# Cumulated decays of a state space scan as selected rows, and where its small copies and scalings run

## What is computed

```python
zxbcdt = jnp.einsum('bld,ed->ble', u, W_in)          # z: 1024, x/B/C: 1024 + 128 + 128, dt: 16 heads
xBC = silu(_causal_depthwise_conv(xBC, conv_w, conv_b))
dt = softplus(dt + dt_bias);  A = -exp(A_log)
def step(h, inp):                                    # h: 16 heads x 64 x 128
    h = h * exp(dt * A)[..] + (dt * x)[..] * B[..]
    y = einsum('bhpn,bn->bhp', h, C)
y = y + D * x
y = y * silu(z)
y = y * rsqrt(mean(y * y) + EPS) * norm_w
return einsum('ble,de->bld', y, W_out)
```

## Time and profile before

| | before |
|---|---|
| median of three runs | 1223.34 us (1223.04 to 1226.01) |
| the profiled execution's own time | 1224.82 us |
| its span | 1223.1 us |
| granted TensorE clock, mean over the span | 0.934 |
| busy: PE, DVE, ACT, POOL | 88%, 70%, 39%, 29% |

### The profile page before, as it was taken

How to read it: one execution, slowest core, us unless ns; L and a number is a source line. 1 busy time by engine, 2 the same in 40 slices (tenths; PEclk the granted TensorE clock), 3 DMA queues, 4 the chain that set the end, 5 groups by cost and what they waited for, 6 DMA issues and landing times.

```text
span 1223.1 us, 14496 instructions
## 1 busy us (share of the span) xinstructions
PE 1072.2 (88%) x4844; PEld 507.3 (41%) x4844; DVE 852.1 (70%) x1164; ACT 471.3 (39%) x706; POOL 354.7 (29%) x166
## 2 busy tenths in 40 slices
PE   7999999699999899789447999999897789996897
PEld 3444444344444344434113444444621144684353
DVE  6577777899999056673862299999366339275696
ACT  2354454566665134136760110100044424334163
POOL 4244544244433013000010377774100000361003
PEclk9999999799999899889768999999979889997898
DMA  6154554432230783020010445453100200000000
GB/s 235 54 168 144 168 177 150 156 106 94 103 103 35 274 310 138 0 87 1 1 69 1 140 158 205 150 206 104 35 1 1 70 2 1 1 1 1 2 1 35
DMA packets 41844, 112.61 MB, mean 92 GB/s; under 512 B 4528, under 2 KB 15312, under 8 KB 35664
## 3 DMA queue, kind: packets, MB, share of 16 engines
q1 hardware_dynamic: 38608, 101.13, 23.7%
q10 hardware_dynamic: 2880, 9.96, 2.4%
q0 software_dynamic: 320, 1.05, 0.3%
HBM read 103.18 MB, written 7.34 MB: 90 GB/s over the span
## 4 chain that ended last, share of the span: by engine, by line
PE 60%; DVE 23%; issue 9%; ACT 7%; DVEq 1%; ACTq 0%; DMA 0%; POOL 0%; SPq 0%; POOLq 0%
PE PS L1502 5%; PE PS L1504 5%; PE PS L1503 5%; PE PS L870 4%; DVE arena L659 3%; PE PS L249 3%; PE PS L250 3%; PE PS L251 3%; PE PS L1570 2%; DVE XN L609 2%; DVE arena L1772 2%; PE PS L744 2%; PE PS L745 2%; PE PS L746 2%; PE PS L1893 1%
## 5 line engine op out<-in xcount | busy, mean ns | idle before, releaser
L714 PE MATMUL PS<-arena 128*128 128x512 f16 x256 | 97.1, 379 | 9.7 <-POOL arena L466 7.6
L744 PE MATMUL PS<-arena 128*128 128x512 f16 x256 | 97.9, 383 | 5.9 <-DVE arena L659 5.9
L491 POOL TENSOR_TENSOR arena<-arena 128x2048 f16<-128x2048 f32 x16 | 70.1, 4381 | 111.4 <-ACT arena L536 105.4
L1502 PE MATMUL PS<-arena 128*128 128x512 f16 x256 | 97.0, 379 | 1.8 <-DVE arena L1393 1.8
L745 PE MATMUL PS<-arena 128*128 128x512 f16 x256 | 97.9, 382 | 0.0
L746 PE MATMUL PS<-arena 128*128 128x512 f16 x256 | 97.8, 382 | 0.0
L715 PE MATMUL PS<-arena 128*128 128x512 f16 x256 | 97.0, 379 | 0.0
L716 PE MATMUL PS<-arena 128*128 128x512 f16 x256 | 97.0, 379 | 0.0
L1503 PE MATMUL PS<-arena 128*128 128x512 f16 x256 | 97.0, 379 | 0.0
L1504 PE MATMUL PS<-arena 128*128 128x512 f16 x256 | 97.0, 379 | 0.0
L659 DVE SCALAR_TENSOR_TENSOR arena<-arena,MASK 128x512 f16<-128x512 f16 (+1 forms) x64 | 96.0, 1500 | 0.1
(11 more groups left out here) (340 smaller groups left out, 2387.0 us busy)
## 6 DMA issues: line engine op xcount, KB each, us to landing
arena<-in_ctxT SPq DMA_DIRECT2D x32, 1024.0 KB, 6.4
arena<-in_ctx SPq DMA_DIRECT2D x16, 1024.0 KB, 5.3
arena<-in_w ACTq DMA_DIRECT2D x8, 1024.0 KB, 5.2
arena<-in_w SPq DMA_DIRECT2D x8, 1024.0 KB, 4.8
XN<-in_ffnGU SPq DMA_DIRECT2D x16, 384.0 KB, 3.3
XN<-in_WinT SPq DMA_DIRECT2D x16, 290.0 KB, 5.0
gu_hi<-arena SPq DMA_DIRECT2D x16, 192.0 KB, 3.4
gu_lo<-arena SPq DMA_DIRECT2D x16, 192.0 KB, 3.5
```

The source lines that it names most:

```text
L714: pe.matmul(bank, CHI[:, b, e, cols], QHI[:, e, :], start=(e == 0), stop=False)
L744: pe.matmul(PS[:, t, :], PHI[:, j, cols], CHI[:, b, j, :], start=False, stop=False)
L1502: pe.matmul(bank, QHI3[:, e, cols], CHI3[:, b, e, :], start=(e == 0), stop=False)
```

## The change

The decays of all heads are first summed over the steps with the heads as rows. POOL fills SELECT, which has for each head a 128-column block with ones in three rows (0, 32 and 64 rows down). DVE copies DTA three times into DTAR, 32 columns apart; four float32 products of PE, now with the two sums ahead of z, put the cumulated decays of the 16 heads, three times, into 96 rows of bank 7. DVE splits them into three bf16 parts (PARTS). In a round, one bf16 product of 512 columns writes the negative numbers for four heads, and for each head one bf16 product of its SELECT block with PARTS adds the decays. ACT, not DVE, copies B. ACT takes a square root of a constant before it waits for the last output, and scales the third and fourth output (after DVE has scaled its first), DVE the first and second. SELECT, PARTS and DTAR have memory of their own; REST lies where the old state's part is kept from the second round on.

```diff
-        DVE_MARK = marks(... "s4_sums_read", "s4_la", "s5_taps", ...)
+        DVE_MARK = marks(... "s4_sums_read", "s4_la", "s4_parts", "s5_taps", ...)
-        POOL_MARK = marks(... "s4_pad", "s4_wout")
+        POOL_MARK = marks(... "s4_pad", "s4_select", "s4_wout")
@@ -1633,6 +1633,10 @@
         LA = view(SMALL + 4096, [3, NT, SSM_H])
         ELA = view(SMALL + 5120, [3, NT, SSM_H])
         NLA = view(SMALL + 2304, [NT, SSM_H])
+        SELECT = view(170 * K, [SSM_H, P], BF16)
+        PARTS = view(174 * K, [N], BF16)
+        DTAR = view(175 * K, [NT, 96])
+        REST = view(159 * K, [N])
         MS = view(SMALL + 3072, [NT])
         RMS = view(SMALL + 3328, [NT])
@@ -1677,6 +1681,15 @@
         def s4_pool(pool, link):
             pool.wait_ge(x_done, NT * 4)
             pool.memset(XBC[:, :, 0:3], 0.0).then_inc(pool_marks, 1)
+
+            link(pool.memset(SELECT, 0.0))
+            for part in range(3):
+                ins = pool.affine_select(out=SELECT, in_=SELECT, compare_op=ALU.not_equal, fill=1.0,
+                                         base=-32 * part, pattern=[[-1, SSM_H], [0, P]], channel_multiplier=1)
+                if part < 2:
+                    link(ins)
+                else:
+                    ins.then_inc(pool_marks, 1)
             pool.wait_ge(act_marks, ACT_MARK["s4_ela"])
             for q in range(NT):
                 if q < NT - 1:
@@ -1732,6 +1745,8 @@
             act.wait_ge(dve_marks, DVE_MARK["s4_la"])
             act.activation(ELA, LA, ACT.Exp).then_inc(act_marks, 1)
             for q in range(NT):
+                act.wait_ge(s4_small, q + 1)
+                act.copy(BNAT, PS[:, 2, 0:P])
                 if q:
                     act.wait_ge(s4_intra, q)
                 for h in range(SSM_H):
@@ -1741,9 +1756,14 @@
                     if h % 4 == 3:
                         ins.then_inc(s4_decay, 1)
             for q in range(NT):
+                if q == NT - 1:
+                    act.activation(COLS[:, 46:47], EPSC[:, 0:1], ACT.Sqrt)
                 act.wait_ge(s4_ys, q + 1)
                 link(act.activation(ZG[:, q, :], YS[:, q, :], ACT.Square, accum_out=MS[:, q:q + 1]))
             act.activation(RMS, MS, ACT.Sqrt, scale=1.0 / SSM_I, bias=EPSC[:, 0:1]).then_inc(act_marks, 1)
+            act.wait_ge(s4_yn, 1)
+            for q in (2, 3):
+                act.activation(YS[:, q, :], YS[:, q, :], ACT.Copy, scale=RMS[:, q:q + 1]).then_inc(s4_yn, 1)
             for c in range(IT):
                 act.wait_ge(s4_yt_psum, c + 1)
                 if c == 0:
@@ -1761,7 +1781,11 @@
             dve.wait_ge(act_marks, ACT_MARK["s4_softplus"])
             link(dve.scalar_tensor_tensor(out=DTV, in0=DTV, scalar=0.0, in1=DTE, op0=ALU.max, op1=ALU.add))
             link(dve.tensor_scalar(ALOG, ALOG, -1.0, None, ALU.mult))
-            dve.tensor_tensor(DTA, DTV, ALOG.unsqueeze(1).to_broadcast([P, NT, SSM_H]), ALU.mult).then_inc(dve_marks, 1)
+            link(dve.tensor_tensor(DTA, DTV, ALOG.unsqueeze(1).to_broadcast([P, NT, SSM_H]), ALU.mult))
+            link(dve.memset(DTAR, 0.0))
+            for part in range(3):
+                ins = dve.tensor_copy(DTAR[:, :, 32 * part:32 * part + SSM_H], DTA)
+            ins.then_inc(dve_marks, 1)
             dve.wait_ge(pool_marks, POOL_MARK["s4_pad"])
             for g in range(CVT):
@@ -1787,6 +1811,14 @@
             link.note(dve.tensor_scalar(NLA, SUMS[:, 0], -1.0, None, ALU.mult))
             link(dve.tensor_tensor(LA[:, 1], SUMS[:, 1], SUMS[:, 0], ALU.subtract))
             dve.sem_inc(dve_marks, 1)
+
+            link(dve.tensor_copy(PARTS[0:96, :], PS[0:96, 7, :]))
+            link(dve.tensor_tensor(REST[0:96, :], PS[0:96, 7, :], PARTS[0:96, :], ALU.subtract))
+            for rows in (slice(32, 64), slice(64, 96)):
+                link(dve.tensor_copy(PARTS[rows, :], REST[rows, :]))
+            rows = slice(64, 96)
+            link(dve.tensor_tensor(REST[rows, :], REST[rows, :], PARTS[rows, :], ALU.subtract))
+            dve.tensor_copy(PARTS[rows, :], REST[rows, :]).then_inc(dve_marks, 1)
             dve.wait_ge(s4_z, 2 * NT)
             for q in range(NT):
@@ -1794,7 +1826,6 @@
                 xs = PS[:, 0:2, :].rearrange("p a (h c) -> p (a h) c", c=SSM_P)
                 dve.tensor_tensor(heads(DTX[:, 0:SSM_I]), xs, DTV[:, q, :].unsqueeze(2).to_broadcast([P, SSM_H, SSM_P]),
                                   ALU.mult).then_inc(s4_dtx, 1)
-                link.note(dve.tensor_copy(BNAT, PS[:, 2, 0:P]))
                 dve.tensor_tensor(heads(YS[:, q, :]), xs, SSMD.unsqueeze(2).to_broadcast([P, SSM_H, SSM_P]),
                                   ALU.mult).then_inc(s4_read, 1)
                 for g in range(4):
@@ -1828,7 +1859,7 @@
             dve.tensor_tensor(YS[:, NT - 1, :], YS[:, NT - 1, :], ZG[:, NT - 1, :], ALU.mult).then_inc(s4_ys, 1)
             dve.wait_ge(act_marks, ACT_MARK["s4_rms"])
             link(dve.reciprocal(RMS, RMS))
-            for q in range(NT):
+            for q in range(2):
                 dve.tensor_scalar(YS[:, q, :], YS[:, q, :], RMS[:, q:q + 1], None, ALU.mult).then_inc(s4_yn, 1)
             for c in range(IT):
                 dve.wait_ge(xt_hi, 2 * DT + c + 1)
@@ -1856,6 +1887,14 @@
                     ins = matmul_split(pe, PS[:, g % 4, :], (WIN_HI[:, c, cols], WIN_LO[:, c, cols]),
                                        (XT_HI[:, c, :], XT_LO[:, c, :]), c, DT)
                 ins.then_inc(s4_conv_psum, 1)
+            pe.wait_ge(dve_marks, DVE_MARK["s4_dta"])
+
+            for k, rows in enumerate((UPPER, ONES)):
+                ins = pe.matmul(PS[:, 6, k * P:(k + 1) * P], rows[:, :], DTVA.rearrange("p t h -> p (t h)"),
+                                start=True, stop=True)
+            for q in range(NT):
+                ins = pe.matmul(PS[0:96, 7, q * P:(q + 1) * P], DTAR[:, q, :], UPPER[:, :], start=True, stop=True)
+            ins.then_inc(pe_marks, 1)
             for g in range(2 * NT):
                 if g >= 2:
                     pe.wait_ge(s4_z, g - 1)
@@ -1865,12 +1904,6 @@
                     ins = matmul_split(pe, PS[:, 4 + half, :], (XT_HI[:, c, rows], XT_LO[:, c, rows]),
                                        (WIN_HI[:, c, cols], WIN_LO[:, c, cols]), c, DT)
                 ins.then_inc(s4_z_psum, 1)
-            pe.wait_ge(dve_marks, DVE_MARK["s4_dta"])
-
-            for k, rows in enumerate((UPPER, ONES)):
-                ins = pe.matmul(PS[:, 6, k * P:(k + 1) * P], rows[:, :], DTVA.rearrange("p t h -> p (t h)"),
-                                start=True, stop=True)
-            ins.then_inc(pe_marks, 1)
             pe.wait_ge(s4_cv, CVT)
             pe.wait_ge(s4_z, 2 * NT)
             for q in range(NT):
@@ -1884,14 +1917,15 @@
                 pe.transpose(PS[:, 2, 0:P], CV[:, IT, cols], IDENT[:, :])
                 pe.matmul(PS[:, 3, 0:P], CV[:, IT, cols], CV[:, IT + 1, cols], start=True, stop=True).then_inc(s4_small, 1)
                 if q == 0:
-                    pe.wait_ge(dve_marks, DVE_MARK["s4_sums_read"])
+                    pe.wait_ge(dve_marks, DVE_MARK["s4_parts"])
+                    pe.wait_ge(pool_marks, POOL_MARK["s4_select"])
                 for g in range(4):
+                    pe.matmul(PS[:, 4 + g, :].rearrange("p (h l) -> p h l", h=4), IDENTB[:, :],
+                              FUTUREB[:, :].unsqueeze(1).to_broadcast([P, 4, P]), start=True, stop=False)
                     for h in range(4):
-                        at = PS[:, 4 + g, h * P:(h + 1) * P]
-                        pe.matmul(at, IDENTB[:, :], FUTUREB[:, :], start=True, stop=False)
-                        ins = pe.matmul(at, DTA[:, q, 4 * g + h:4 * g + h + 1].to_broadcast([P, P]), UPPER[:, :],
-                                        start=False, stop=True)
+                        ins = pe.matmul(PS[:, 4 + g, h * P:(h + 1) * P], SELECT[0:96, 4 * g + h, :],
+                                        PARTS[0:96, q * P:(q + 1) * P], start=False, stop=(h == 3))
                     ins.then_inc(s4_decay_psum, 1)
                 pe.wait_ge(s4_read, q + 1)
                 if q:
```

More of the change, by code:

```diff
@@ L170, in perceiver_kernel @@
         PE_MARK = marks("s0_turned", "s0_spread", "s0_close", "s0_den", "s1_mean", "s1_var", "s1_spread", "s4_dt_psum", "s4_sums", "s5_scale_psum")
-        DVE_MARK = marks("s0_mask", "s0_colmax", "s0_o", "s1_rstd", "w_scale", "s3_memidx", "s4_dtb", "s4_dta", "s4_sums_read", "s4_la", "s5_taps", "s5_scale",
+        DVE_MARK = marks("s0_mask", "s0_colmax", "s0_o", "s1_rstd", "w_scale", "s3_memidx", "s4_dtb", "s4_dta", "s4_sums_read", "s4_la", "s4_parts", "s5_taps", "s5_scale",
                           "s5_out_scale")
         ACT_MARK = marks("s1_std", "s3_mks_hi", "s4_softplus", "s4_ela", "s4_rms")
-        POOL_MARK = marks("s0_primed", "const_ready", "s1_wall", "s3_primed", "s3_iota", "s3_ones", "s4_pad", "s4_wout")
```

(1 more changed line is left out.)

## The result

With the change, the kernel takes 1217.89 us (median of five, 1216.42 to 1218.73) against 1223.34 (1223.04 to 1226.01): ratio 0.9948, interval 0.9937 to 0.9959. It is faster, inside the forecast's range, and 3.5 us above its point of 1214.4. The profiled execution took 1216.42 us, the fastest of the five, for a span of 1214.7.

A forecast was written before the change was run, and what follows sets the result against it. TensorE was taken to bound the rounds, its decays only back to VectorE's last bank read. Terms +0.15 - 1.05 (first round, front included) - 7.0 - 1.27 + 0.25 = -8.9 us from 1223.34 gave 1214.4; range 1211.8 to 1219.0.

The forecast's parts named there:

- The rounds: State space rounds: shorter decays save 2.60 us in the second, 2.20 in third and fourth, together 7.0.
- BNAT on ScalarE: In each round, moving B's copy from VectorE to ScalarE lets VectorE's last bank read end 0.20 us earlier.
- VectorE's front: Before the rounds: a memset, three small copies and a wait ahead of VectorE's convolution cost 0.95 us (0.7 to 1.3).
- The tail: Behind the rounds: early square root table load saves 1.27 us, shared scaling costs 0.25.
- the sharing: Last four scalings split between VectorE and ScalarE: costs 0.25 us, between 0 and 0.4.
- L212 and the fills: Early stage: GpSimd's first SELECT fill delays VectorE's L212 by 0.15 us, between 0 and 1.9.
- The stall in z: TensorE's 3.05 us wait for ScalarE's first SiLU of z hides 1.4 us of moved and added products, costing nothing.
- The clock rival: TensorE loses its clock in the rounds: 26 us slower, total 1240; chance 0.05.
- this rival: Rounds: GpSimd's split of output weights meets VectorE's L1822, up to 2.14 us in two rounds, +4.3, total 1218.7; chance 0.10.
- the rival of the long fills: GpSimd's SELECT fills exceed 1.9 us and hold VectorE's work from 1009.98 on: +3.5, total 1217.9; chance 0.09.
- the last rival: Rounds: decay products don't shrink to 0.055 us but take 0.22 each; sum -3.3, total 1220.0; chance 0.08.
- The forecast's own bounds: Spread from front, scaling, second round and runs 3 us apart: -11.5 to -6.5 us, without the rivals.

The follow-up runs named there:

- e7: Changed kernel with B's copy back on VectorE, no early square root and no shared scaling (decays alone): 1219.19 us, ratio 0.9962 to the kernel before.
- e4: Kernel before with only B's copy on ScalarE, the early table load and the shared scaling, decays as before: 1222.09 us, ratio 0.9984.
- e5: Changed kernel with GpSimd's fills of SELECT begun only after TensorE turned the last layer norm tile: 1216.21 us, ratio 0.9932 to the kernel before.
- e8: Changed kernel with two SiLUs of z ahead of the last convolved tile, late SELECT fills, all four scalings on VectorE: 1209.88 us, ratio 0.9884.
- e12: Changed kernel with VectorE's memset of DTAR standing three times, to lengthen TensorE's stall in z: 1218.54 us, ratio 0.9948 to the kernel before.
- e1: Changed kernel again, unedited, for a second profile: 1217.48 us against 1224.39 for the kernel before, ratio 0.9945.
- e3: Changed kernel with ScalarE's first two SiLUs of z ahead of the last convolved tile, removing the stall: 1214.44 us, ratio 0.9915 to the kernel before.
- e2: Changed kernel with 36 unread float16 products on TensorE ahead of the wait in z: 1214.24 us, ratio 0.9925 to the kernel before.

## Why the prediction was right, and where it was off

- **The rounds: right.** -2.61, -2.21 and -2.22 for -2.60, -2.20 and -2.20. The step that did it was not the products' price but the bound: L1899 can't start before VectorE's last read, so the gain is 2.20 and not the 3.56 that TensorE gets. After, the bracket of L1933 names exactly that read. That the sizes meet to 0.02 us is in part luck: in the third round L1933 starts 4.68 us behind L1849, not 4.79, and L1849 comes 7.38 behind L1933, not 7.28. The decays' price from the earlier trace rows held too: four groups that step at 0.44 to 0.45, for 4 x 0.44 = 1.76, with 1 us to spare.
- **BNAT on ScalarE: right.** 0.20 a round (e7), hidden where the decays are long (e4).
- **VectorE's front: right.** +0.96 for 0.95. The stall became shorter (2.28; forecast near 2.7, and e5, where dt isn't late, has 2.69). That it ended at 1040.27, near the forecast's 1040.6, is a coincidence: L212 came 1.60 us earlier and dt was 1.16 later than reckoned.
- **The tail: right.** -1.11 for -1.02: the load gone, the sharing +0.23 for +0.25 (8.60 against e8's 8.37). Sharing the scalings as the change does costs; it doesn't gain.
- **L212 and the fills: the first step that failed.** "so L212 at 998.85 rather than 998.71: +0.15" is what L212 did (0.70). But the term ended there. The dt products behind it run just where TensorE's clock comes up, at 0.72 before and 0.50 after, and the term measured 1.31 (e5).
- **The stall in z: the second.** "Against it: in 1031 to 1040 TensorE stalled 3.05 us in one piece, busy 5.95 of 9, and the clock stayed 1.00." The row is right, and was read as a rule: a stall of this length costs no clock. The change's own stall refutes it, shorter at 2.28 and 1.53 us dearer, and so does e12 with 3.33. The clock rival was weighed for the rounds, where it did not come, and not for the place where the change moved a stall: the same stall that "hides what TensorE gets" cost 1.53.
- **The rivals.** L1716 (L1703 before) ends at 1093.27 and L1853 (L1822) starts at 1093.39, 1.22 long: they passed each other by 0.12 us, so this rival was missed by as little as the forecast's 0.13. What a meeting costs, two rows early in the program show, in the trace of before:

```profile
24.02 4.28 POOL L466 TENSOR_TENSOR arena<-arena 128x2048 f16<-128x2048 f32 x1 [0.18 <-POOL arena L477]
```

```profile
24.41 4.44 DVE L579 TENSOR_TENSOR X<-X,arena 128x512 f32<-128x512 f32 x1
28.89 0.69 DVE L579 TENSOR_TENSOR X<-X,arena 128x512 f32<-128x512 f32 x1
```

The first L579 here (X and a bias, both in SBUF) ran beside GpSimd's L466 and ended 0.55 us behind it; the next one, alone, took 0.69. The rule of the Trainium skill (SBUF — State Buffer, section Who interferes with whom) says so of a VectorE instruction with two SBUF inputs beside a GpSimd one that reads SBUF, and these rows agree. As for the rival of the long fills, they took 8.28 us (995.17 to 1003.45) and ended before VectorE's work from 1009.98 on, which it named; the four L289 that run beside the selects took 2.48 us, before and after. Against the last rival, the products did shrink; its price leaves out the front's 0.95, which a first round that gains nothing would have left as a cost.

- **The range: partly luck.** The forecast's own bounds (-11.5 to -6.5) reach to 1216.8, and the median is 1217.89. It lies in the range only because this was widened to 1219.0 for two rivals that did not come. The clock, which did come at two places, had a price of 26 us for the rounds and stood outside the range.

With both terms at their measured size the sum is -8.9 + 1.16 + 1.53 = -6.2. The medians show -5.4 (the result) and -6.9 (e1). The 0.58 us by which the profiles differ behind the turn is no part of that sum.

## What to carry to other kernels

Shortening the bound engine's work is worth only the distance to the next thing that its successor waits for; find that row first, and price the gain by it. Then go through every place where the change shifts a pause of TensorE, however little, and price the products behind it at both clock levels. A pause that is to stay can be filled with products that nobody reads, but reordering the queue that causes it gains more (e3 against e2 at the turn: 43.53 and 45.96; the medians, 1214.44 and 1214.24, don't tell them apart).

## What was not expected of the hardware

- Behind a pause of 2.3 us TensorE ran at the lower level for some 3.3 us (1040.27 to 1043.54; mean clock 0.57 over 1040 to 1044), though the clock had been 1.00 from 1031 to 1040, the first 2 us of the pause included; behind 2.69 us (e5) it began at full speed and slowed a microsecond later. Behind 3.05 us (before) and 3.04 (e4) it stayed at 1.00. What tells these apart is open.
- A delay of 0.15 us ahead of a chain of 48 short products cost 1.31 us: they ran at the lower level from first to last, where before the last 21 had run at full speed.
- Beside GpSimd's memset of 128x2048 bf16 (1.82 us) a VectorE row of 0.55 took 0.70, while the four rows beside its selects of that size (6.32 for three) took no longer than before.
